# A graph layer with a mixture of experts: half a tile of nodes moves from the gathered to the dense part

## What is computed

```python
def reference(x, src, dst, edge_weight, ...):
    xn = layernorm(x)                                   # 3125 x 256
    agg = segment_sum(xn[src] * edge_weight[:, None], dst, 3125)
    x = x + agg @ W.T + b
    h = layernorm(x)
    shared = relu(relu(h @ sW1 + sb1) @ sW2 + sb2) @ sW3 + sb3
    all_out = [relu(relu(h @ eW1[e] + eb1[e]) @ eW2[e] + eb2[e]) @ eW3[e] + eb3[e] for e in 4]
    gates = softmax(h @ gW + gb); topv, topi = top_k(gates, 2); topw = softmax(topv)
    return x + shared + sum(topw * all_out[topi])
```

## Time and profile before

| what | us |
| --- | --- |
| median of 3 runs | 438.51 |
| lowest and highest run | 437.15, 439.93 |
| profiled execution: its time | 439.22 |
| profiled execution: its span | 437.4 |
| PE, POOL, VectorE, ACT busy | 352.9, 310.8, 234.2, 156.3 |

### The profile page before, as it was taken

One profiled execution on the slowest core, in us unless ns is written; L12 is line 12 of the kernel. 1 busy time (PEld: TensorE's weight loads), 2 busy tenths in 40 slices (PEclk: granted clock), 3 DMA queues, 4 the chain that ended last, 5 costly groups with the idle time before them and its releaser, 6 DMA issues.

```text
span 437.4 us, 7466 instructions
## 1 busy us (share of the span) xinstructions
PE 352.9 (81%) x2410; PEld 286.9 (66%) x2410; DVE 234.2 (54%) x905; ACT 156.3 (36%) x330; POOL 310.8 (71%) x319
## 2 busy tenths in 40 slices
PE   0004287798999898977999999979999987998985
PEld 0002256686887786865788688758878864966874
DVE  7899979973335782773633247733520451522441
ACT  1544625422322552452124125423420233253461
POOL 7776877787777777777777777777777777777200
PEclk9999779999999999998999999998999999999989
DMA  6994754434444424343433343343434333434200
GB/s 180 371 346 134 188 140 101 100 97 106 105 127 108 109 87 130 99 122 108 121 98 108 105 124 96 97 123 107 133 103 128 108 102 104 128 102 126 72 1 29
DMA packets 48962, 53.31 MB, mean 122 GB/s; under 512 B 27819, under 2 KB 38810, under 8 KB 48922
## 3 DMA queue, kind: packets, MB, share of 16 engines
q0 software_dynamic: 14784, 40.39, 31.0%
q1 hardware_dynamic: 30442, 9.14, 9.0%
q10 hardware_dynamic: 3696, 3.28, 2.2%
HBM read 46.30 MB, written 6.48 MB: 121 GB/s over the span
## 4 chain that ended last, share of the span: by engine, by line
POOL 63%; issue 20%; PE 7%; DMA 5%; DVE 2%; SPq 1%; ACT 1%; POOLq 0%; DVEq 0%
POOL rows L714 63%; DMA x_sb<-in_x 4%; PE hid_ps L1031 2%; SPq L598 1%; PE tok_ps L1072 1%; PE window_ps L933 1%; DMA rows<-normalised_rows,src_all 1%; PE agg_ps L951 1%; PE tok_ps L1061 1%; PE tok_ps L1070 1%; DMA normalised_rows<-xn_all 0%; PE hid_ps L1040 0%; PE tok_ps L1073 0%; PE agg_ps L996 0%; PE hid_ps L1044 0%
## 5 line engine op out<-in xcount | busy, mean ns | idle before, releaser
L714 POOL DMA_INDIRECT rows<-normalised_rows,src_all x284 | 285.6, 1006 | 89.0 <-issue 89.0
L933 PE MATMUL window_ps<-rows,select 128*32 128x256 f32 x616 | 42.6, 409 | 35.2 <-DMA rows<-normalised_rows,src_all 24.8
L980 PE MATMUL agg_ps<-dense,xn_all 128*128 128x256 f32 (+1 forms) x300 | 63.7, 360 | 0.0
L980 PEld LDWEIGHTS agg_ps<-dense,xn_all 128*128 128x128 f32 x300 | 52.8, 190 | 6.1 <-issue 1.2
L933 PEld LDWEIGHTS window_ps<-rows,select 128*32 128x32 f32 x616 | 20.9, 115 | 50.6 <-issue 33.1
L1031 PE MATMUL hid_ps<-xt,ew_sb 128*128 128x256 f32 (+2 forms) x224 | 48.4, 362 | 0.0
L840 ACT ACTIVATE h<-hid_ps,b_sb 128x256 f32<-128x256 f32 (+2 forms) x84 | 32.9, 443 | 41.6 <-PE hid_ps L1031 40.4
L1362 DVE TENSOR_TENSOR select<-slots,rel 128x384 f32<-128x384 f32 (+1 forms) x26 | 14.3, 550 | 59.4 <-PE window_ps L933 59.4
L1031 PEld LDWEIGHTS hid_ps<-xt,ew_sb 128*128 128x128 f32 x224 | 39.2, 195 | 6.0 <-issue 1.8
L782 ACT ACTIVATE windows<-window_ps 128x256 f32<-128x256 f32 (+1 forms) x26 | 10.0, 384 | 75.0 <-PE window_ps L933 71.9
L698 POOL DMA_INDIRECT rows<-in_x,src_first x24 | 23.1, 960 | 7.2 <-issue 6.9
(11 more groups left out here) (146 smaller groups left out, 576.7 us busy)
## 6 DMA issues: line engine op xcount, KB each, us to landing
rows<-normalised_rows,src_all POOLq DMA_INDIRECT x284, 2.8
x_sb<-in_x SPq DMA_DIRECT2D x6, 512.0 KB, 10.1
normalised_rows<-xn_all ACTq DMA_DIRECT2D x6, 512.0 KB, 7.3
out<-y SPq DMA_DIRECT2D x10, 256.0 KB
records<-in_rec SPq DMA_DIRECT2D x144, 1.5 KB
ew_sb<-in_ew SPq DMA_DIRECT2D x1, 512.0 KB
out<-y SPq DMA_DIRECT2D x4, 128.0 KB
rows<-in_x,src_first POOLq DMA_INDIRECT x24, 3.9
```

The costliest lines, as they stand in the source:

```text
L714: pool.indirect_dma_start(rows[:, b % RING * BATCH + pos, :], None, table[:, :], bass.IndirectOffsetOnAxis(ap=src_all[:, c:c + 1], axis=0) ...
L933: last = pe.matmul(window_ps[SLOT * g:SLOT * (g + 1), 0:D], select[:, b % RING, j, :], rows[:, b % RING * BATCH + pos, :], start=(i == 0), ...
L980: last = pe.matmul(dense_ps[:, k * PAIR:k * PAIR + tok], xn_all[:, h, k * P:(k + 1) * P], dense[:, h, 0:tok], start=(h == 0 and k == 0), s ...
```

## The change

The border between the two parts moves by half a tile, from node 2432 to node 2368. The gathered part has 300 chunks in place of 308: 25 full batches and no 26th. G10 has 64 nodes in place of 128. The dense units begin at nodes 2368, 2624 and 2880 with 256, 256 and 245 nodes, in place of 256, 256 and 181 nodes that began at whole tiles. Since they now straddle tiles, their rows are loaded a second time into `x_sb`, shifted by half a tile (`load_shifted`, five DMAs of SP behind the weights), and the first dense unit's bias waits for them. A unit's first node is a field of its own (`at`). Stores of units with an incomplete tile are cut at a multiple of 16 rows. The constants of `schedule()` are also changed: ranks, number of open units, parts of the row normalisation. The arithmetic is the same. The diff, cut to its core:

```diff
-G_TILES = 19
-G_NODES = G_TILES * P
+HALF = P // 2
+G_TILES = 18
+G_NODES = G_TILES * P + HALF
...
-GATHERED += [Unit("G", 9, 17, 1, P), Unit("G", 10, 18, 1, P)]
-DENSE = [Unit("D", 0, 19, 2, PAIR), Unit("D", 1, 21, 2, PAIR), Unit("D", 2, 23, 2, P + TAIL)]
+GATHERED += [Unit("G", 9, 17, 1, P, 17 * P), Unit("G", 10, G_TILES, 1, HALF, G_TILES * P)]
+DENSE = [Unit("D", v, G_TILES + 1 + 2 * v, 2, min(PAIR, N_NODES - G_NODES - v * PAIR), G_NODES + v * PAIR)
+         for v in range(3)]
...
-PARTS, OPEN, BANKS = 6, 2, 2
-NEAR, BEHIND, HURRY, FIRST = 0.1, 0.5, 2.0, 1
-COUNT_BEHIND, STATS_BEHIND = 2, 0
+PARTS, OPEN, BANKS = 3, 3, 2
+NEAR, BEHIND, HURRY, FIRST = .2, 1.2, 1.0, 0.3
+BUILD, MULT, LATE = 1.2, 0.6, 0.0
+COUNT_BEHIND, STATS_BEHIND = 4, 3
...
-                            at("sums", DENSE[v - 1]) if v and k % BANKS else 0.0), 6, ("build", k), 1.1)
+                            at("sums", DENSE[v - 1]) if v and k % BANKS else 0.0), BUILD, ("build", k), 1.1)
...
-                      7, ("mult", v, h), 0.865 * DENSE[v].tok / PAIR)
+                      MULT, ("mult", v, h), 0.865 * DENSE[v].tok / PAIR)
...
+            def load_shifted():
+
+                for unit in DENSE:
+                    whole = unit.tok // P
+                    sp.dma_start(x_sb[:, unit.tile:unit.tile + whole, :],
+                                 x[unit.at:unit.at + whole * P, :].rearrange("(t p) d -> p t d", p=P)
+                                 ).then_inc(s_shifted, 16)
...
                     if what == 1:
                         load_weights()
+                        load_shifted()
...
+                if unit.kind == "D" and unit.i == 0:
+                    dve.wait_ge(s_shifted, 16 * sum(stores_of(v) for v in DENSE))
```

More of the change, by code:

```diff
@@ L53 @@
 FAR = 1.0e6
-Unit = namedtuple("Unit", "kind i tile T tok")
-GATHERED = [Unit("G", 0, 0, 1, P)] + [Unit("G", i, 2 * i - 1, 2, PAIR) for i in range(1, 9)]
-GATHERED += [Unit("G", 9, 17, 1, P), Unit("G", 10, 18, 1, P)]
-DENSE = [Unit("D", 0, 19, 2, PAIR), Unit("D", 1, 21, 2, PAIR), Unit("D", 2, 23, 2, P + TAIL)]
+Unit = namedtuple("Unit", "kind i tile T tok at")
+GATHERED = [Unit("G", 0, 0, 1, P, 0)]
+GATHERED += [Unit("G", i, 2 * i - 1, 2, PAIR, (2 * i - 1) * P) for i in range(1, 9)]
+GATHERED += [Unit("G", 9, 17, 1, P, 17 * P), Unit("G", 10, G_TILES, 1, HALF, G_TILES * P)]
+DENSE = [Unit("D", v, G_TILES + 1 + 2 * v, 2, min(PAIR, N_NODES - G_NODES - v * PAIR), G_NODES + v * PAIR)
+         for v in range(3)]
 WINDOWS = [-(-u.tok // WIN) for u in DENSE]
@@ L86, in batches_of @@
 def batches_of(u):
[L87 removed]
+    lo, hi = u.at, u.at + u.tok
     step = STEP * BATCH
@@ L148, in unit_steps @@
     def unit_steps(u):
-        q, T, half = units.index(u), u.T, u.tok / PAIR
+        q, T, half = units.index(u), u.T, max(0.42, u.tok / PAIR)
         one = units[q - 1] if q else None
@@ L298, in schedule @@
             ready = [(can_open(waiting[kind][0]), kind) for kind in "DG" if waiting[kind]]
-            ready = [(t, kind) for t, kind in ready if t is not None and t <= min(free[e] for e in ("pe", "act", "dve")) + 1.0]
+            ready = [(t + (LATE if kind == "D" else 0.0), kind) for t, kind in ready
+                     if t is not None and t <= min(free[e] for e in ("pe", "act", "dve")) + 1.0]
             if ready:
@@ L577, in rows_of, with rest_of @@
             return [min(unit.tok - t * P, P) for t in range(unit.T)]
+        def rest_of(unit):
+            rest = unit.tok % P
+            return [(lo, hi) for lo, hi in ((0, rest // 16 * 16), (rest // 16 * 16, rest)) if hi > lo]
         def stores_of(unit):
-            return 1 if unit.tok % P == 0 else 2
+            return (unit.tok >= P) + len(rest_of(unit))
         def stores_before(n):
@@ L649, in store @@
                 sp.wait_ge(s["y"], n + 1)
[L650 to L655, removed]
+                whole, at = unit.tok // P, unit.at
+                if whole:
+                    sp.dma_start(out[at:at + whole * P, :].rearrange("(t p) d -> p t d", p=P),
+                                 u.y[:, 0:whole, :]).then_inc(s_out, 16)
+                for lo, hi in rest_of(unit):
+                    sp.dma_start(out[at + whole * P + lo:at + whole * P + hi, :],
+                                 u.y[lo:hi, whole, :]).then_inc(s_out, 16)
+            def load_shifted():
[4 more added lines that the diff above has]
+                                 ).then_inc(s_shifted, 16)
+                    for lo, hi in rest_of(unit):
+                        sp.dma_start(x_sb[lo:hi, unit.tile + whole, :],
+                                     x[unit.at + whole * P + lo:unit.at + whole * P + hi, :]
+                                     ).then_inc(s_shifted, 16)
             load_records(0)
@@ L944, in merge @@
                     pe.wait_ge(s["x1"], n)
-                lo_node = unit.tile * P
+                lo_node = unit.at
                 for b in mine:
@@ L1214, in count_smaller @@
             def count_smaller(v):
-                first = DENSE[v].tile * P
+                first = DENSE[v].at
                 if v:
@@ L1550, in fetch_sums @@
                     dve.wait_ge(s["lin"], q - 1)
-                at = unit.tile * P
+                at = unit.at
                 dve.tensor_copy(sums[q % 2][:, :, 0:unit.tok],
```

3 lines of the change are left out of this document (2 added, 1 removed).

## The result

The changed kernel takes 451.81 us (median of 4 runs, 449.64 to 454.88), the kernel before 439.22 in the same comparison (437.15 to 440.68, 4 runs). The ratio is 1.0284, with a 95% interval of 1.0234 to 1.0334: slower by 2.8%. The forecast was 450.0 us, in a range of 445 to 456. The profiled execution took 450.89 us with a span of 449.1, against 439.22 and 437.4 before: +11.7 us in both.

The account below looks back on a forecast made before the run. POOL's gather pace was taken to bound the kernel up to batch 24, then PE's list behind it. Terms −1.4 + 3.7 + 6.3 − 0.5 − 0.3 + 2.0 + 0.8 + 0.9 = +11.5 us gave 450.0 us, range 445.0 to 456.0.

Parts of the forecast that it names:

- The bound: POOL's gathers set the pace up to batch 24, the last PE waits for; then PE's list, 34.8 us, sets the end.
- PE on time at batch 24: Ahead of batch 24 PE has only 0.8 us more work, so it is on time: cost 0, at most +4 us.
- The added work: PE's extra dense work: builds +3.4 us, D2's multiplication +5.9, D2's layers +1.5, together +10.8 us ahead of the last batch.
- What stands behind the batch: In PE's list behind batch 24: D2's layer 3, +3.7 us, and G8's logits and layer 1, +6.3 us, no longer covered.
- Spread and layer 3 of G8: PE's waits at these two steps lose their cover behind batch 24: +0.9 us, bounds 0 and 1.3.
- `lin` of G10: It comes right behind G10's merge, so the copy of the sums is bare: +0.8 us, bounds 0 and 1.1.
- The wait at G9's layer 2: PE waits while ACT does G10's root and G9's exponential with two table loads: +2.0 us, bounds 0 and 3.1.
- −1.4 for batch 25: Batch 25 disappears from PE's list at the end, saving 1.4 us; its gathers' 10.5 us on POOL were already hidden.
- the shorter merge: G10's merge on PE reads two batches in place of three, four records less: −0.5 us.
- The gathers' time: Rival: the gathers are the bound, so their 10.5 us come off and the kernel takes about 428 us; chance 3%.
- The two cancel: Rival: added work finds idle time, waits stay covered or a faster POOL brings batch 24 forward: 438 to 440 us; 4%.
- PE the bound in the middle: Rival: part of PE's added 10.8 us finds no slack, batch 24 begins 3 to 6 us late: 453 to 456 us; 18%.

Follow-up runs that it names:

- e6: The kernel before without the eight gathers of batch 25 (its sums come from old rows): 439.13 us against 439.09, ratio 0.999.
- e8: The changed kernel with D2's multiplication at 181 columns in place of 245 (64 columns of sums left out): 455.78 us, ratio 1.0308 to the kernel before.
- e3: The changed kernel's new border with other, searched constants of the order: 441.58 us, ratio 1.0021 to the kernel before; 1.0503 when repeated in a slower session.
- e4: The changed kernel with D2's layer 3 moved back ahead of batch 24 in PE's list: 451.05 us, ratio 1.023 to the kernel before.
- e5: The changed kernel with G10's square root moved on ACT back behind G9's layer 1: 460.67 us, ratio 1.0374 to the kernel before.
- e1: The changed kernel's new border with the order constants of the kernel before: 448.25 us, ratio 1.0191 to the kernel before.
- e7: The changed kernel without the five loads of shifted rows (dense residuals read other rows): 452.01 us, ratio 1.023 to the kernel before.

## Why the prediction was right

*The bound.* POOL's pace up to the last awaited batch, then PE's list: shown. The last gather starts at 397.1 and the batch at 400.00, as forecast ("near 397", "near 400 after a wait"). e6 shows directly that nothing behind it on POOL counted.

*PE on time at batch 24.* Right, it waited 2.24 us, and e8 shows it from the other side. The reason given for it holds too: ahead of the batch PE should have about as much work as before, and from 140 to 400 us it is busy for 236.2 us against 236.7. Ahead of 140 us it is busy for 5.6 us more (91.0 against 85.4), of which I had foreseen 0.8; its clock was lower there too (granted share 0.91 from 60 to 140 us, 1.00 before), and the waits for batches took it up. The added work was sized in part: the multiplication of D2 went from 16.7 us to 22.5, +5.8 for a forecast +5.9, by these groups of the changed kernel, which answer to the earlier trace rows:

```profile
L1006 PE MATMUL agg_ps<-dense,xn_all 128*128 128x245 f32 x100 | 22.5, 371 | 0.0
L994 PE MATMUL build_ps<-high_node,low_1h 128*128 128x125 f32 x154 | 23.4, 300 | 0.0
L994 PE MATMUL agg_ps<-high_node,low_1h 128*128 128x125 f32 x152 | 21.5, 287 | 2.6 <-DVE high_node L1444 2.5
```

The builds grew by more than the forecast 3.4 us: by 3.3 in the group of the earlier trace rows alone, and in both groups from 39.7 to 44.9 us, 5.2. One of the 306 records now costs 0.147 us against the 0.14 that I reckoned with. None of it shows in the start of batch 24.

*What stands behind the batch.* D2's layer 3 took 402.72 to 406.31, 3.6 us (forecast 3.7). G8's logits and the three parts of layer 1 took 0.81 + 1.81 + 1.81 + 1.73 = 6.2 us, by the starts of the rows that follow them (forecast 6.3). This is the heart of the result, and e3 confirms it: in an order that has both ahead of the batch, the time is that of the kernel before. e4 adds the condition: the list ahead must have the room, for D2's layer 3 alone put back gained 0.5 us.

*The waits.* Spread and layer 3 of G8 waited 0.51 and 0.63, 1.1 us together. I had forecast +0.9, with 0.4 set off as waited before; PE's timeline of the kernel before shows no wait at these steps (404.92 and 406.88), so that it is +1.1. `lin` of G10 waited 0.37 (forecast +0.8). I had read 0.8 us of bare wait between G9's merge and its `lin`, but G8's spread stood between them on PE. The wait at G9's layer 2 was the term that I sized wrong: +2.0 forecast, with 2 to 3 us of idle time as its sign, and it is 1.62 against 0.72 before, +0.9. The row of the kernel before, from PE's timeline:

```profile
418.48 0.71 PE L1040 MATMUL hid_ps<-h,sw_sb 128*128 128x128 f32 x4 [0.72 <-ACT h L840]
```

I had counted two table loads where the list that I showed has one: G9's root had left its table in place, and G10's root took 0.3 us. ACT's timeline of the changed kernel:

```profile
427.63 0.29 ACT L839 ACTIVATE std<-mv,eps 128x1 f32<-128x1 f32 x1
427.94 1.28 ACT L853 ACT_TABLE_LOAD   x1
```

And the step itself was half wrong: I wrote the root's new place down as a loss, but e5 shows that the old place costs about 3 us more in this list. With one root after the other and one exponential after the other ACT loads fewer tables: two behind batch 24 in the changed kernel, four in the kernel before.

*What I had not in the sum* is the clock, about 2.2 us net. I had named it for the upper end of the range only. Batch 24 took 2.79 us in place of 1.50, and the last layer 3 took from 442.15 to the result at 445.87, 3.7 us, in place of 432.24 to 434.27, 2.0 us; with G10's spread it is 3.5 us, of which the 1.3 us that the low clock had cost before go off.

*Luck.* The forecast of 11.5 us and the measured 11.5 agree in part by luck. The terms of the sum, without the clock, came to about 9.4: −1.4 for batch 25, +3.6, +6.2, −0.4 for the shorter merge, +0.9, +0.4 and +1.1 for the three waits make 10.4, and the remaining −1.0 fell to G10 and to other waits that got shorter (the one at its turn went from 1.03 us to 0.46), for which I had −0.3. The clock, which was no term, made up for the 2 us that the sum had too much, about half of it in the table load counted twice.

*The rivals.* The gathers' time, refuted by e6. The two cancel: they did not, though e3 shows that they can, by another order and not by a faster POOL (its last gather started at 398.45). PE the bound in the middle: not in this order, but in e1, with the old constants, PE is 2 us late.

## What to carry to other kernels

When a producer with a steady pace feeds an engine that works through a fixed list, ask which delivery is the last that is waited for, and then sum up what the list holds behind it. A saving on the producer behind that point is worth nothing, and work added ahead of it is free while it fits into the waits; work moved from ahead of it to behind it is paid in full. A change of the split must therefore be judged together with the order that the scheduler makes of it: here the same split cost 2.8% or nothing, by the constants of the scheduler. And before a difference of a few microseconds is put down to the order, look at the granted clock of both traces: here the low clock cost between nothing (e6) and more than 4 us (e3) of a tail, and 1.3 us in the kernel before.

## What the hardware showed

The granted clock of PE in the tail of the changed kernel, by stretches (start and end, length, then busy time of PE, its weight loads, VectorE, ACT and POOL, then the granted clock as a share of 2.4 GHz, the DMA share and GB/s):

```profile
399.50:402.80 3.30, 2.80 (x25) 1.22 (x25) 0.00 (x0) 0.00 (x0) 0.00 (x0) 0.50 0.02 5
402.80:440.30 37.50, 33.14 (x208) 27.65 (x208) 14.95 (x70) 13.78 (x40) 0.00 (x0) 1.00 0.06 18
440.30:446.30 6.00, 4.79 (x12) 2.60 (x12) 0.93 (x3) 0.55 (x3) 0.00 (x0) 0.51 0.02 5
```

In the searched order of e3 the low level lay where layer 2 of G9 had waited:

```profile
419.50:429.70 10.20, 9.65 (x39) 7.96 (x40) 3.26 (x19) 2.01 (x9) 0.00 (x0) 0.51 0.00 1
```

It is 1.2 GHz in the stretches with 0.50 or 0.51, and 2.4 between. After a wait of 2.24 us at batch 24 PE ran the 24 records of the batch in 2.79 us in place of 1.50, in the changed kernel, in e5 (wait 2.31) and in e8 (wait 2.15); after a wait of 1.90 (e3) or 0.78 us (e7) the batch took 1.50. Not each longer wait did this: batches behind waits of 2.97 and 3.81 us elsewhere in the changed kernel took 1.50 and 1.61, and one behind a wait of 4.69 took 2.79. Nor did the same list bring the same clock: behind the wait of 1.62 us at G9's layer 2 the clock stayed high in the changed kernel and was low from 432.9 to 439.7 us in e4. From what the traces show I can say what a low stretch cost, but not when one will come. The table load on ACT took 1.28 us and, where its operand was ready, the next activation began 0.01 to 0.02 us after its end.
